# Slots of a hand-laid instruction order changed in a one-core gated attention and mixture kernel

## The reference

```
z    = layernorm(x)                      # over the 2048 columns
q, k = Wq z + bq, Wk z + bk              # 256 rows each
v    = Wv ctx + bv
p    = softmax(q^T k / sqrt(32), masked) # in each window of 128, by head
o    = gelu(v p^T)
x    = x + tanh(g_x) (Wo o + bo) * mask
s    = softmax(router(layernorm(x)))     # 64 experts, the 8 largest kept
x    = x + tanh(g_f) (layernorm(x) * sum(s) + s @ expert_bias)
```

## Time and profile before

| | us |
|---|---|
| median of 3 runs | 1180.27 |
| the 3 runs | 1179.55, 1180.27, 1185.96 |
| the profiled execution | 1178.47 |
| its span, first to last instruction | 1176.7 |
| mean granted TensorE clock, share of full speed | 0.993 |

### The profile page before, as it was taken

One profiled execution on the slowest core, in us unless ns is written; L12 is line 12 of the kernel. 1 busy time (PEld: TensorE's weight loads), 2 busy tenths in 40 slices (PEclk: granted clock), 3 DMA queues, 4 the chain that ended last, 5 costly groups with the idle time before them and its releaser, 6 DMA issues.

```text
span 1176.7 us, 32708 instructions
## 1 busy us (share of the span) xinstructions
PE 1122.1 (95%) x11661; PEld 1041.6 (89%) x11661; DVE 947.1 (80%) x1833; ACT 1028.7 (87%) x3200; POOL 719.8 (61%) x684
## 2 busy tenths in 40 slices
PE   2899999999999999999999999999999999999976
PEld 2798999899998999899998999989999899989965
DVE  6868878988789977889778887889778997787767
ACT  3798989989999899988999989999899989999954
POOL 2675767467655667566764676747765667655621
PEclk9899999999999999999999999999999999999989
DMA  9468454786547954588456765478554785556433
GB/s 289 110 171 216 112 136 114 249 208 156 135 121 257 229 133 121 151 249 210 125 132 215 210 178 134 122 248 234 128 131 124 254 230 135 127 173 172 112 83 144
DMA packets 160162, 199.39 MB, mean 169 GB/s; under 512 B 26496, under 2 KB 102272, under 8 KB 159872
## 3 DMA queue, kind: packets, MB, share of 16 engines
q1 hardware_dynamic: 158848, 196.80, 61.2%
q10 hardware_dynamic: 1152, 0.50, 0.2%
HBM read 79.67 MB, written 33.65 MB: 96 GB/s over the span
## 4 chain that ended last, share of the span: by engine, by line
PE 63%; DVE 11%; SPq 7%; ACT 7%; issue 4%; POOL 3%; DMA 3%; ACTq 0%; DVEq 0%; POOLq 0%
PE ring L308 8%; PE ring L310 7%; PE ring L309 7%; SPq L519 7%; PE ring L365 4%; PE ring L348 4%; ACT T L616 4%; PE ring L384 4%; PE ring L386 4%; PE ring L385 4%; PE ring L323 3%; PE ring L325 3%; PE ring L324 3%; PE ring L403 3%; PE ring L453 2%
## 5 line engine op out<-in xcount | busy, mean ns | idle before, releaser
L616 ACT ACTIVATE T<-ring,nmx 128x128 f32<-128x128 f32 x1024 | 359.6, 407 | 29.9 <-DVE nmx L772 28.9
L308 PE MATMUL ring<-z_hi,wqk_hi 128*128 128x256 f32 x1024 | 298.4, 291 | 26.0 <-DVE z_lo L954 21.8
L310 PE MATMUL ring<-z_lo,wqk_hi 128*128 128x256 f32 x1024 | 291.3, 284 | 0.0
L309 PE MATMUL ring<-z_hi,wqk_lo 128*128 128x256 f32 x1024 | 291.1, 284 | 0.0
L616 ACT ACTIVATION_READ_ACCUMULATOR T<-ring,nmx 128x1 f32 x1024 | 252.2, 247 | 0.0
L1044 POOL TENSOR_TENSOR z_lo<-z,z_hi 128x1024 fp32r<-128x1024 f32 x62 | 147.7, 2382 | 161.9 <-ACT z_hi L584 161.9
L308 PEld LDWEIGHTS ring<-z_hi,wqk_hi 128*128 128x128 f32 x1024 | 197.1, 193 | 38.6 <-DVE wqk_lo L930 21.8
L778 DVE STREAM_TRANSPOSE T<-T 128x512 f32<-128x512 f32 x256 | 169.8, 691 | 45.2 <-ACT T L616 44.8
L1056 POOL TENSOR_TENSOR X<-X,xt 128x512 f32<-128x512 f32 x128 | 165.8, 1295 | 56.3 <-DVE xt L805 56.1
L310 PEld LDWEIGHTS ring<-z_lo,wqk_hi 128*128 128x128 f32 x1024 | 197.6, 193 | 0.0
L309 PEld LDWEIGHTS ring<-z_hi,wqk_lo 128*128 128x128 f32 x1024 | 197.4, 193 | 0.0
(11 more groups left out here) (134 smaller groups left out, 2672.2 us busy)
## 6 DMA issues: line engine op xcount, KB each, us to landing
PT<-T SPq DMA_DIRECT2D x1018, 80.0 KB, 2.2
X<-in_x SPq DMA_DIRECT2D x64, 512.0 KB, 5.6
cx<-in_ctx SPq DMA_DIRECT2D x128, 256.0 KB, 3.9
out_y<-X SPq DMA_DIRECT2D x128, 256.0 KB, 3.1
mg<-in_mask SPq DMA_DIRECT2D x64, 128.0 KB, 3.6
sel<-rows_d SPq DMA_DIRECT2D x128, 3.0 KB
X<-in_eb SPq DMA_DIRECT2D x2, 512.0 KB, 8.6
X<-in_wqT SPq DMA_DIRECT2D x1, 512.0 KB, 4.8
```

The lines of the kernel that those rows point to most:

```text
L308: e.matmul(o, wqk_hi[:, t, cols], z_hi[:, t, :], t == 0, False)
L309: e.matmul(o, wqk_lo[:, t, cols], z_hi[:, t, :], False, False)
L310: last = e.matmul(o, wqk_hi[:, t, cols], z_lo[:, t, :], False, t == DT - 1)
L616: last = e.activation(T[u % 2][:, :, n, :], bank("S", 4 * u + g)[:, k * W:(k + 1) * W].rearrange("p (b j) -> p b j", b=4), ACT.Exp, bias=n ...
```

## The change

It gives new slots to `mv` (8.5 to 9.5), `xt` (the step `weigh_out`, 29.75 to 29.25), `R` (`r_mm`), `LT` (`c_turn`), `c_w` (`c_weights`) and `mix`, changes shifts of the last three units and adds some, and makes the loops of `S` (`scores`), `q`, `k`, `q_ev`, `k_ev` and `top` heed shifts. No instruction is added, removed or changed in size. Read out in full, the lists differ so:

- SP and GpSimd: not at all.
- At each of the 7 batch ends (shown for batch 4): VectorE runs `weigh_out(41,0)` ahead of `add_mix` (4,0,0) in place of after (4,0,1). TensorE runs `scores(43)` ahead of `mix` (4,2,1) in place of behind it, `r_mm(40,0)` ahead of `mix` (4,3,0) and `r_mm(40,1)` ahead of (4,3,1), in place of ahead of (4,3,2) and (4,3,3).
- TensorE in the last units: `scores(63)` ahead of `project_out(61,0)`, and `weigh(62)` ahead of `r_turn(61)`.
- VectorE: `top(63)` ahead of `weigh_out(61,0)`, `turn_p(63,0)` ahead of `weigh_out(61,1)`.
- ScalarE: `q_full(61)` ahead of `r_high(58)`, `v_full(126)` ahead of `o_high(61)`, `q_full(63)` ahead of `r_high(60,1)`.
- Bank claims: many steps get another bank. In plain units `project` q now claims after `weigh_out` and `v_mm` after `v_full`, the other way round than before; at batch ends the four claims of `scores` wait for the adds 3 to 6 in place of 4 to 7.

```diff
--- before.py
+++ after.py
@@ -45,13 +45,13 @@
 
     c_hi=-15.5, c_lo=-13.75, v=-10.75, v_ev=-7.5, v_gap=-3.25,
 
-    S=-1.75, top=1, exp=4, e_gap=0.25, tp=6.25, td=7.25, mv=8.5, PV=25.25, on=23.25,
-
-    gelu=23, mg=2, ot_hi=24, ot_lo=27.5, WO=27.25, WO_gap=5.75, xt=29.75, x1=31, bn2=39.25,
-
-    hT=37.5, hT_gap=0.25, ht_hi=41.25, ht_lo=41.75, R=47.25,
-
-    norm2=27.5, L=36, LT=34, c_top=38.75, c_exp=37.75, c_w=40.75, c_sc=40.75, wT=43, wt_hi=43.25, wt_lo=42.25, mix=43.75, m_gap=0.25,
+    S=-1.75, top=1, exp=4, e_gap=0.25, tp=6.25, td=7.25, mv=9.5, PV=25.25, on=23.25,
+
+    gelu=23, mg=2, ot_hi=24, ot_lo=27.5, WO=27.25, WO_gap=5.75, xt=29.25, x1=31, bn2=39.25,
+
+    hT=37.5, hT_gap=0.25, ht_hi=41.25, ht_lo=41.75, R=47,
+
+    norm2=27.5, L=36, LT=35, c_top=38.75, c_exp=37.75, c_w=40.25, c_sc=40.75, wT=43, wt_hi=43.25, wt_lo=42.25, mix=44, m_gap=0.25,
     sx=44.75, sx_gap=1.25, x2=45.25, rl=50.75, rl_gap=5,
 
     x_1=21, x_gap=7, bn1=65.75, bn1_gap=2.25, norm1=101.25,
@@ -59,11 +59,14 @@
 
 
 ENDS = {
-    ("exp", 1): -8, ("tp", 1): -1.75, ("td", 1): -0.25, ("mv", 1): 15, ("PV", 1): -2.75, ("on", 1): -2,
-    ("gelu", 1): 2, ("ot_hi", 1): 4.5, ("ot_lo", 1): -4.75, ("WO", 1): -2.5, ("xt", 1): -1, ("x1", 1): 1.5,
-    ("bn2", 1): -0.25, ("hT", 1): -3.75, ("ht_hi", 1): 3.5, ("ht_lo", 1): -1.25, ("R", 1): -11.5,
-    ("gelu", 2): -2.25, ("ot_hi", 2): 1, ("ot_lo", 2): -1, ("WO", 2): 4.25, ("xt", 2): 0.25, ("x1", 2): -2,
-    ("hT", 2): 1, ("ht_hi", 2): 8.75, ("ht_lo", 2): 1.75, ("hT", 3): -2.75, ("ht_hi", 3): 6.75, ("ht_lo", 3): 2.5, ("bn2", 3): 1, ("R", 3): 3.5,
+    ("exp", 1): -8, ("tp", 1): -2.25, ("td", 1): -0.75, ("mv", 1): 15, ("PV", 1): -2.75, ("on", 1): -1,
+    ("gelu", 1): 2, ("ot_hi", 1): 5.5, ("ot_lo", 1): -4.75, ("WO", 1): -2.5, ("xt", 1): -1, ("x1", 1): 1.5,
+    ("bn2", 1): -1.25, ("hT", 1): -3.25, ("ht_hi", 1): 0.5, ("ht_lo", 1): -1.25, ("R", 1): -11.5,
+    ("gelu", 2): -2.5, ("ot_hi", 2): 1, ("ot_lo", 2): -3, ("WO", 2): 3.75, ("xt", 2): 1.25, ("x1", 2): -1.5,
+    ("hT", 2): 1, ("ht_hi", 2): 8.75, ("ht_lo", 2): 1.75, ("hT", 3): 0.25, ("ht_hi", 3): 6.75,
+    ("ht_lo", 3): 2.5, ("bn2", 3): 1, ("R", 3): 3.5, ("top", 2): 2, ("x1", 3): -0.25, ("S", 1): -4,
+    ("top", 1): -4, ("mv", 2): -2.5, ("ot_hi", 3): 1, ("q_ev", 1): -0.25, ("q_ev", 3): -1, ("PV", 2): -4,
+    ("exp", 2): -1.5, ("xt", 3): 1, ("bn2", 2): 0.25,
 }
 
 
@@ -252,13 +255,13 @@
             free.append((t + round(8 * held), i, freed_by, n))
 
         for t in TICKS:
-            for u in due(t, C["S"]):
+            for u in units(t, "S"):
                 for g in range(4):
-                    take(("S", 4 * u + g), t, end("exp", u) + C["e_gap"] * (g + 1) - C["S"], exp_a, 4 * u + g + 1)
-            for u in due(t, C["q"]):
-                take(("q", u), t, C["q_ev"] - C["q"], q_a, u + 1)
-            for u in due(t, C["k"]):
-                take(("k", u), t, C["k_ev"] - C["k"], k_v, u + 1)
+                    take(("S", 4 * u + g), t, end("exp", u) + C["e_gap"] * (g + 1) - end("S", u), exp_a, 4 * u + g + 1)
+            for u in units(t, "q"):
+                take(("q", u), t, end("q_ev", u) - end("q", u), q_a, u + 1)
+            for u in units(t, "k"):
+                take(("k", u), t, end("k_ev", u) - end("k", u), k_v, u + 1)
             for w in range(2):
                 for u in due(t, (8 + C["v_gap"]) * w + C["v"]):
                     take(("v", 2 * u + w), t, C["v_ev"] - C["v"], v_a, 2 * u + w + 1)
@@ -723,7 +726,7 @@
-                for u in due(t, C["q_ev"]):
+                for u in units(t, "q_ev"):
                     q_full(u)
...
@@ -983,14 +986,14 @@
-                for u in due(t, C["top"]):
+                for u in units(t, "top"):
                     top(u)
...
-                for u in due(t, C["k_ev"]):
+                for u in units(t, "k_ev"):
                     k_full(u)
```

## The result

The median of 13 runs after is 1176.34 us (1169.66 to 1177.64), against 1179.66 of 13 runs before (1176.57 to 1187.17). The ratio is 0.9948 with a 95% interval of 0.9928 to 0.9968: 6.1 us less, between 3.8 and 8.5, so the kernel after is faster, by a little. The profiled execution after took 1176.34 with a span of 1174.5, which is 2.2 less than the span before. Five of the 13 runs after lie at 1169.7 to 1173.4 and eight at 1175.9 to 1177.6; the medians are therefore only 3.3 apart, and I go by the ratio.

The account below looks back on a forecast made before the run. TensorE, busy 95% of the span, was taken as the bound. Batch ends 5.6 plus last units 2.5 give 8.1 us; 1178.47 - 8.1 = 1170.4, plus 1.1 gives 1171.5 us, 8-in-10 range 1168.0 to 1177.5.

Parts of the forecast that it names:

- SP's order: Moving the `mv` slot leaves SP's instructions in the same order: cost nothing, gain nothing.
- The change of banks in plain units: In plain units `project` q and `v_mm` claim banks freed well ahead of them; costed at nothing.
- Rival 3: The change does not do what it says: SP's order stays, the value lay there, nothing is left; 1179.6, chance 0.10.
- One batch end: From the first `mix` to `project_out` j=1, TensorE gains 1.06 us; each batch end is worth 0.6 to 1.06.
- the 14th add: Bank claim of `project_out(41,1)` at a batch end, ready at 778.3 at the least; taken as just met at 779.11.
- The term for the seven: The seven batch ends at 0.8 us each give 5.6 us, bounds 4.2 and 7.4.
- The margin of `weigh(43)`: Behind a batch end, the 0.6 between the last copy landing and `weigh(43)` starting would be nearly gone.
- rival 1: Waits pass to later `mix` steps or next units' copies, so only the last units gain; 1177.1, chance 0.14.
- The end: The last units up to `weigh(63)` gain 2.5 us, between 1.0 and 2.9; the chain behind is left alone.
- The part of the forecast that rested on the clock: The second clock drop, before `project_out(62,0)`, goes away; the stretch to `weigh(63)` is up to 1.6 us shorter.
- Rival 2: The lower clock after idle time before `weigh(62)` comes later, covers next steps; last units give 0.5; 1173.5, chance 0.10.
- rival 4: Slower: `weigh(62)`, ahead of `r_turn(61)`, and TensorE's work behind it wait for SP's sixteenth copy; 1184.9, chance 0.04.

Follow-up runs that it names:

- `weigh_out` alone: The kernel before with only `weigh_out` j=0 ahead of the first add on VectorE at the seven batch ends; median 1176.10 us, ratio 0.9947.
- `scores` alone: The kernel before with only `scores` and `r_mm` earlier among TensorE's `mix` steps at the seven batch ends; median 1185.94 us, ratio 1.0015.
- the batch ends alone: The kernel before with only the change's orders and bank claims at the seven batch ends, last units as before; median 1176.55 us, ratio 0.9944.
- small loads: Loads of `x` for batches 2 to 7 cut to 16 of 1024 columns; ratio 0.9952 in the kernel before, 0.9911 in the kernel after.
- the fastest kernel: The kernel after with `c_low` first, and a second half-load of `x` one step earlier in SP's order, ahead of `load_ctx`; 1165.40 us, ratio 0.9855.
- `c_low` first: On GpSimd `c_low` put ahead of `z_full` of a batch's first unit; ratio 0.9962 in the kernel before, 0.990 in the kernel after.
- the last units alone: The kernel before with only the change's orders of the last units, batch ends as before; median 1177.95 us, ratio 0.9965.
- the filler run: The kernel after with eleven unread matmuls in TensorE's idle time ahead of `weigh(62)`; median 1176.04 us, ratio 0.9949.
- the load behind `move`: The kernel after with the second load of the batch after next issued behind the copies of `move(8b+3)`, 6 times; 1204.37 us, ratio 1.018.

## Why the prediction was right, and where its sizes were off

The direction and the mechanism held: 1171.5 was forecast, within 1168.0 to 1177.5; measured is a median of 1176.34, and by the ratio 1179.66 x 0.9948 = 1173.5. That is 0.52%, just about what I had called the bound of what can be told from no change, and the interval of the ratio lies wholly below 1. The forecast of 8.1 us lies within the interval, 3.8 to 8.5, near its far end.

**SP's order.** It was said not to change, and it didn't. That `mv`=9.5 does nothing by itself is borne out by the kernel with the slot put back. The change of banks in plain units shows no wait of `project` or `v_mm` in the waits of after, as costed. Rival 3 falls, since the value did not lie in that step.

**One batch end.** Forecast was 1.06 us for TensorE; measured 0.93 at batch 4 from the first `mix`, and 0.90 as the mean of seven up to `weigh` (0.82 at batch 4). VectorE's idle time before the first add came to 0.28 (forecast 0.3). `top(43)` came 0.46 earlier, counted from the first `mix` (0.6). Most of the missing 0.13 is the 14th add, which I had taken as just met: after the ninth add VectorE waits twice, 0.24 for a product and 0.38 for a scaling, so the 14th ends at about 777.60, and `project_out(41,1)`, which claims its bank, starts at 777.66. The term for the seven, 5.6, was low at its place: 7 x 0.90 = 6.3. The margin of `weigh(43)` did shrink, from 0.69 to 0.21 us, as worked out.

The Trainium skill (Perfetto Trace Analysis, Optimization Strategy) says that a gap that repeats on the engine that should be saturated can mean that there is not enough SBUF or PSUM for the next tile. Taken as the prediction took it, the batch ends would have given nothing. The run with `weigh_out` alone shows 0.79 us at each from the order on VectorE, with as many banks and with `scores` still waiting for the adds 4 to 7; the run with `scores` alone shows what happens where the order on the draining engine stays: the waits stand elsewhere. So a lack of banks did not decide this gap, the 1.22 us of VectorE did.

**The waits handed on (rival 1).** I kept it as an alternative with 0.14. At their places the change's pieces measure 6.3 for the batch ends and 3.4 for the end (below), 9.7 together; alone they measured 6.6 and 4.1; the whole measured 6.1 (3.8 to 8.5), and the same lists a second time 7.4 (4.7 to 10.3). So the whole may well be less than its pieces, but no run shows it beyond the noise.

The traces show where time went in the executions that they caught. In the pair before and after, the six batch ends between `weigh(10)` and `weigh(61)` leave 0.1 of 5.4. Take the row of the copies off that stretch, and 883.49 - 3.90 = 879.59 before stands against 883.42 - 8.64 = 874.78 after: 4.8 less. With the batch ends alone it is 874.92, with small loads 878.80 and 874.65, and in the fastest kernel, which has no such row, 874.77. So the gain of the batch ends is there in each of these traces with the new batch end, and in this pair the waits for copies took it up. That they do so in general is not shown. Over the traces without an edit of SP's surroundings, the six with the shorter batch end have 7.9 to 12.3 us in that row (8.6, 9.6, 10.2, 10.8, 7.9, 12.3), three of the four with the old one 3.9 to 4.7, and the fourth, `scores` alone, 10.4; the kernel before with `c_low` first has 8.4. Three of the high ones are from executions 3.5 to 6.4 us above their kernel's median, and the batch ends alone had 9.6 in the row and the full 6.6 in the time. What is shown, by times, is that the copies bound the kernel next: with the two holds of SP ahead of them taken away in turn, the 0.9948 of the change goes to 0.990 and 0.9855, and the kernel before with the first alone to 0.9962. With both holds out of the way the row is gone and the same stretch is 8.7 us shorter than before (883.49 to 874.77).

So no step of the sum failed, but its sizes were off, and in part cancelled. Both terms were low at their places (5.6 for 6.3, 2.5 for 3.4), and the sum, 8.1, was above the whole. I had allowed 0.26 at each batch end (1.06 to 0.8) for the margin of the one `weigh` behind it, and did not ask what the other `weigh` steps of the batch do when TensorE arrives earlier at all of them. Of each 15.9 us of a unit SP spends 10 to 12 issuing the sixteen copies, as the earlier trace rows show too, so it has little room to follow.

**The end.** `weigh(61)` to `weigh(63)` is 26.37 before and 23.86 after, 2.5 as forecast; `weigh(61)` to `weigh(62)` gained 0.98 (forecast 1.0). Behind it I had said that the chain is left alone, and that one half-clock stretch would stand in place of two. There are two in the trace of after: `weigh(63)` to the first `mix` of batch 7 went from 22.90 to 24.08, with the stretch at 0.50 at 1149.3. Over all traces the end is better than this pair shows: F is 63.69, 65.26, 65.18, 64.57, 64.56 and 65.66 with the old order, mean 64.8, and 62.39, 61.87, 60.77, 60.79, 60.82, 61.90, 60.62 and 62.33 with the new one, mean 61.4. That is 3.4 us, and all of it lies ahead of `weigh(63)`, above the upper bound of 2.9 that I had there: the trace of before, which I sized it by, has the shortest end of the six with the old order. Of its half-clock time 3.4 us lie at `weigh(62)`, while in the other five 6.8 us on end lie around `project_out(62,0)`.

The part of the forecast that rested on the clock was right in its reason and lucky in its case. The second stretch at half clock, behind `project_out(62,0)`, does cost about 1.1 us (I had up to 1.6), and it went away in six of the eight traces with the new order, not in all. The first one, which I left in place, costs nothing there, since the copies of `move(63)` set `weigh(63)`.

**Rivals 2 and 4.** Rival 2 said that the lower clock comes a little later and covers the next steps as well. In the trace of after it did not, though one farther on, at 1149.3, took 1.2 us; in those of the last units alone and of `c_low` first it did, and these ends still gained, with F at 61.87 and 61.90. `weigh(62)` waited 2.78 for its sixteenth copy, and no landing was late enough for rival 4.

**Open.** Why single large waits for copies (1.5 to 3.5 us, at units 8b+3 to 8b+5) come in some traces and not in others. How much of the 17.1 us of the fastest kernel would be there without this change: the kernel before with `c_low` first gives 4.5, and with the load ahead as well it was not run. Whether the whole is less than its two halves, and why the runs after fall in two groups some 5 us apart.

## What to carry to other kernels

Where TensorE waits for banks, look at the engine that drains them, and for work of it that stands behind an idle time it could fill: one step put there gave 0.79 us at each of seven places, while moving the waiting step alone gave 0.1. A saving is only worth its place if the next bound follows, so read the queue that issues small copies: two steps with waits ahead of sixteen copies in an in-order queue cost more than the gaps that the change closed (0.93% against 0.52%), but a load moved behind them the wrong way cost 21 us. Judge a gain by the times of many runs and its place by traces: one profiled execution lay 6.4 us above its kernel's median, more than the whole change is worth. A stretch at the lower clock costs only if TensorE's work is what ends last there.

## What the runs showed of the hardware that I had not expected

- The lower clock does not follow idle time as simply as I had read from three cases. Idle times of 2.48 and 2.36 before, and 2.78 after, stand ahead of a stretch at 0.50; those of 2.39 in the filler run and of 2.39 and 2.26 before `weigh(62)` in two other traces stand ahead of one at 1.00; and in after an idle time of 1.39 stands ahead of one at 0.50, where before has 1.38 at the same place and runs on at 1.00. From `weigh(61)` to the end, without a last stretch that every trace has in its final 5 us, the six traces with the old order spent 6.8 us (three of them) or 10.2 us (three) at half clock; those with the new one 3.4 (five), 6.8 (two) or none (the filler).
- A late copy can cost more than its wait. In the middle, waits for copies of 1.76, 2.29, 2.37, 2.43, 2.66, 3.03 and 3.47 us had such a stretch of 3.4 us right at their end or up to 1.5 us behind it (from 264.0 to 821.4 us, in six traces); others of up to 1.94 had none. In the kernels with the new batch end, that with the load behind `move` left out, the stretch from `weigh(10)` to `weigh(61)` without the row of the copies is 874.7 to 874.9 us with no stretch at 0.50 in it and 876.2 to 876.3 with one: 1.5 us more.
- SP needs 10 to 12 us to issue sixteen copies of one unit, 0.59 us each in the median, of the 15.9 us that a unit takes. A queue that moves few bytes can be nearly as full as TensorE.
- Cutting the loads of `x` of six batches, 174 to 147 GB/s in the mean between 194 and 1110 us, gave 0.4 to 0.5% and left the copies' waits about as they were (3.9 and 4.1, 8.6 and 7.9 us).
